# Quantised layer at four slots a tile beside projections at every second slot, without unread products

## The reference

```python
h = tok(x)                        # relu(x W0') * (x W1'), then Wo', 256 -> 512 -> 256
h = ln(h + attn0(h))              # 16 heads of 16, mask |i - j| <= 64, softmax
h = ln(h + ffn0(h))               # quantised: gate, up (256 -> 1024), down (1024 -> 256)
h = ln(h + attn1(h))              # 16 heads of 16, causal
h = ln(h + moe(h))                # 8 experts (256 -> 1024 -> 256), top 2, then its own layer norm

def act_quant(x):                 # by row
    scale = 127.0 / clip(max(abs(x)), EPS)
    return clip(round(x * scale), -128, 127) / scale
def weight_quant(w):
    scale = 1.0 / clip(mean(abs(w)), EPS)
    return clip(round(w * scale), -1, 1) / scale
def ffn0(x):
    g, u = bitlinear(x, w_gate), bitlinear(x, w_up)
    return bitlinear(square(relu(g)) * u, w_down)
# moe: softmax of x wg, top 2, a running count per expert gives each row its place, at most CAP rows each
```

## Time and profile before

| | |
|---|---|
| Median of 3 runs | 1079.14 us (1068.04 to 1080.44) |
| The profiled execution | 1079.0 us |
| Its span, first to last instruction | 1077.1 us |
| Busy: PE, DVE, ACT, POOL | 914.4, 546.3, 417.6, 295.2 us |
| Mean granted TensorE clock | 0.926 |

### The profile page before, as it was taken

The page is one execution under the profiler, slowest core; times in us unless marked ns, Lnnn a source line. Parts: engine busy times, 40 slices in busy tenths (PEclk is TensorE's granted clock), DMA queues, the critical chain, the costliest instruction groups (busy, mean ns, idle before and its releaser), DMA issues. The chain is left out here.

```text
span 1077.1 us, 14453 instructions
## 1 busy us (share of the span) xinstructions
PE 914.4 (85%) x5031; PEld 561.6 (52%) x5054; DVE 546.3 (51%) x2104; ACT 417.6 (39%) x717; POOL 295.2 (27%) x364
## 2 busy tenths in 40 slices
PE   6897999878879879888987979867999999999940
PEld 3454455534535534434533525344687777777830
DVE  1257434678778678757785767541021112111137
ACT  1315334476475566565635545501311211121003
POOL 5101322413413413301324342335021122112232
PEclk9998999999989999988988988978999999999975
DMA  9882341542253252430564360153142353243242
GB/s 352 146 186 31 32 80 21 60 40 35 27 60 38 32 52 36 48 38 2 60 88 72 38 104 21 57 196 97 40 96 52 118 132 66 77 123 69 25 102 78
DMA packets 57511, 81.49 MB, mean 76 GB/s; under 512 B 6624, under 2 KB 51041, under 8 KB 55008
## 3 DMA queue, kind: packets, MB, share of 16 engines
q1 hardware_dynamic: 49520, 70.48, 32.9%
q0 software_dynamic: 7296, 9.47, 5.2%
q10 hardware_dynamic: 624, 0.63, 0.2%
HBM read 35.37 MB, written 19.68 MB: 51 GB/s over the span
## 5 line engine op out<-in xcount | busy, mean ns | idle before, releaser
L1099 DVE CUSTOM_DVE_ANT_0 junk<-ps,maskb 128x256 bf16<-128x256 f32 (+4 forms) x512 | 206.3, 434 | 96.6 <-PE ps L809 93.2
L630 ACT ACTIVATE probs<-ps 128x512 f32<-128x512 f32 (+1 forms) x304 | 159.2, 550 | 118.5 <-PE ps L832 115.4
L1551 PE MATMUL ps<-dxT,qs 128*128 128x320 f32 x512 | 139.6, 433 | 1.3 <-DVE dxT L1617 1.3
L1563 PE MATMUL ps<-ks,hTe 128*128 128x256 f32 x640 | 139.3, 379 | 0.0
L1587 ACT ACTIVATE hTe<-ps,qs 128x640 f32<-128x640 f32 x64 | 50.8, 794 | 204.6 <-PE ps L1551 204.6
L1563 PEld LDWEIGHTS ps<-ks,hTe 128*128 128x128 f32 x640 | 121.3, 190 | 16.1
L1507 POOL DMA_INDIRECT mixed_rows<-ysb,ids x40 | 61.7, 1543 | 228.8 <-DVE ysb L1637 225.9
L832 PE MATMUL ps<-qs,ks 99*128 99x256 bf16 (+4 forms) x512 | 104.1, 289 | 23.4 <-DVE nmax L1099 13.7
L1551 PEld LDWEIGHTS ps<-dxT,qs 128*128 128x128 f32 x512 | 97.2, 190 | 41.5 <-DVE dxT L1617 1.7
L809 PE MATMUL ps<-ks,qs 96*128 96x256 bf16 (+4 forms) x512 | 106.2, 290 | 11.1 <-DVE nmax L1099 5.4
L848 PE MATMUL ps<-probs,vaug 128*32 128x256 f32 (+4 forms) x1024 | 92.2, 434 | 10.5 <-issue 5.7
(11 more groups left out here) (183 smaller groups left out, 1242.3 us busy)
## 6 DMA issues: line engine op xcount, KB each, us to landing
qs<-parts SPq DMA_DIRECT2D x96, 128.0 KB, 4.7
ks<-parts SPq DMA_DIRECT2D x96, 128.0 KB, 7.4
qs<-w SPq DMA_DIRECT2D x8, 1024.0 KB
ks<-w SPq DMA_DIRECT2D x8, 1024.0 KB, 4.9
dispatched_rows<-att SPq DMA_DIRECT2D x8, 650.0 KB, 16.9
ks<-dispatched_rows SPq DMA_DIRECT2D x4, 650.0 KB, 7.4
x_sb<-xT SPq DMA_DIRECT2D x8, 256.0 KB, 4.2
mixed_rows<-h SPq DMA_DIRECT2D x4, 512.0 KB
```

What stands on the lines that cost most here:

```text
L630: act.activation(probs_of(u)[:, heads[0]:heads[-1] + 1, :], turned_bank((u, half, i))[:, 0:len(heads) * w].rearrange("p (j n) -> p j n", n=w),
L1099: ins = dve.tensor_tensor_reduce(out=junk[:, AT["s", (u, half, i)][0], a * (hi - lo):(a + 1) * (hi - lo)], in0=score_bank((u, half, i))[:, ...
L1551: ins = mm(bank(2 * (n % 2) + c)[:, 0:HC], w1s[:, e % 2, k, m * P:(m + 1) * P], dxT[:, e % 2, k, c * HC:(c + 1) * HC], start=(k == 0), sto ...
L1563: ins = mm(bank(4 + n % 2)[:, 0:D], hTe[:, e % 2, m, t * P:(t + 1) * P], w2s[:, e % 2, m, :], start=(m == 0), stop=(m == MH - 1))
```

## The change

The quantised layer's tiles come four slots apart instead of two, and VectorE reads an up product one slot after TensorE makes it. Projections 2 to 7 take every second slot (`stretched`) and start 8 or 10 slots earlier, so that they run beside the quantised layer (3 to 6), the token layer (2) and the sends (7). The values get a third buffer, and `junk` loses the place of the bank that it never uses. All of `keep_busy` and the six products ahead of the experts go; where the wait stood behind them it now stands ahead of opening the bank.

```diff
+NV = 3
 DENSE = (
-    ("wq", 2, 12), ("qkv", 1, 14), ("tok", 2, 22), ("tok", 3, 34), ("qkv", 2, 46), ("o", 0, 54), ("ffn", 0, 60),
-    ("qkv", 3, 77), ("o", 1, 85), ("ffn", 1, 91), ("qkv", 4, 108), ("o", 2, 117), ("ffn", 2, 123), ("qkv", 5, 140),
-    ("o", 3, 149), ("ffn", 3, 155), ("qkv", 6, 172), ("o", 4, 181), ("gate", 0, 185), ("route", 0, 187), ("send", 0, 196), ("qkv", 7, 204), ("o", 5, 213),
...
+    ("wq", 2, 12), ("qkv", 1, 14), ("tok", 2, 22), ("tok", 3, 34), ("qkv", 2, 38), ("o", 0, 54), ("ffn", 0, 60),
+    ("qkv", 3, 66), ("o", 1, 85), ("ffn", 1, 91), ("qkv", 4, 98), ("o", 2, 117), ("ffn", 2, 123), ("qkv", 5, 130),
+    ("o", 3, 149), ("ffn", 3, 155), ("qkv", 6, 162), ("o", 4, 181), ("gate", 0, 185), ("route", 0, 187),
+    ("send", 0, 196), ("qkv", 7, 196), ("o", 5, 213), ("gate", 1, 217), ("route", 1, 219), ("send", 1, 228),
...
-STEPS = {"tok": 12, "qkv": 8, "o": 6, "ffn": 16, "gate": 2, "route": 9, "send": 4, "bias": 2, "wq": 4}
-FQT, FIRST_TILE, PER_TILE = 3, 3, 2
-QUANT, TURN, DOWN, STATS, NORM = 2, 3, 4, 5, 6
+STEPS = {"tok": 12, "qkv": 8, "o": 6, "ffn": 25, "gate": 2, "route": 9, "send": 4, "bias": 2, "wq": 4}
+FQT, FIRST_TILE, PER_TILE = 3, 3, 4
+HIDDEN = 1
+QUANT, TURN, DOWN, STATS, NORM = 4, 6, 7, 8, 9
+def stretched(phase, i, c):
+    return 2 * c if phase == 'qkv' and 2 <= i else c
-        SCHED.setdefault(_at + _c, []).append((_phase, _i, _c))
+        SCHED.setdefault(_at + stretched(_phase, _i, _c), []).append((_phase, _i, _c))
-            vaug = sb2("vaug", [P, 2, NT, VW])
+            vaug = sb2("vaug", [P, NV, NT, VW])
-            junk = sb2("junk", [P, BANKS, S], BF16)
+            junk = sb2("junk", [P, BANKS - 1, S], BF16)
 # ScalarE, values of a projection
-                                if i < 2:
-                                    act.wait_ge(prep_pool, 8)
+                                if i < NV:
+                                    act.wait_ge(prep_pool, 6 + NV)
+                                elif k == 0:
+                                    act.wait_ge(pv_mm, NG * NT * (i - NV + 1))
 # ScalarE, scaling of a tile
-                            t = tile_at(c, 1)
+                            t = tile_at(c, HIDDEN + 1)
 # TensorE
-                            if u == 0 and half == 0:
-                                pe.wait_ge(mask_done, 1)
-                                keep_busy(o, 24)
...
-                            o = d_open(("ffn", i, "fqT"))
-                            keep_busy(o, 12)
-                            o = o.bitcast(BF16)
                             pe.wait_ge(fq_done, i + 1)
+                            o = d_open(("ffn", i, "fqT")).bitcast(BF16)
...
-                                o = d_open(("ffn", i, f"f{t}"))
-                                keep_busy(o, 3)
-                                o = o.bitcast(BF16)
                                 pe.wait_ge(fq2_done, NT * i + t + 1)
+                                o = d_open(("ffn", i, f"f{t}")).bitcast(BF16)
...
+                            pe.wait_ge(chosen, i + 1)
                             o = d_open(("route", i, "cnt"))
-                            keep_busy(o, 10)
-                            pe.wait_ge(chosen, i + 1)
...
-                            if i == 0:
-                                keep_busy(o, 12)
                             pe.wait_ge(w_sum, i + 1)
...
-                    pe.wait_ge(routed, B)
-                    keep_busy(bank(V_BANK), 34)
 # VectorE
-                            t = tile_at(c, 0)
+                            t = tile_at(c, HIDDEN)
                             if t is not None:
                                 hidden(i, t, 0)
-                            t = tile_at(c, 1)
+                            t = tile_at(c, HIDDEN + 1)
                             if t is not None:
                                 hidden(i, t, 1)
                                 hidden_scale(i, t)
 # TensorE, experts
-                    for _ in range(6):
-                        mm(bank(0), identb[:, :], maskb[:, 0:S], start=True, stop=True)
```

More of the change, by code:

```diff
@@ L97 @@
     ("tok", 0, -20), ("qkv", 0, -8), ("tok", 1, 0), ("bias", 0, 1), ("bias", 1, 2), ("wq", 0, 4), ("wq", 1, 8),
-    ("wq", 2, 12), ("qkv", 1, 14), ("tok", 2, 22), ("tok", 3, 34), ("qkv", 2, 46), ("o", 0, 54), ("ffn", 0, 60),
-    ("qkv", 3, 77), ("o", 1, 85), ("ffn", 1, 91), ("qkv", 4, 108), ("o", 2, 117), ("ffn", 2, 123), ("qkv", 5, 140),
-    ("o", 3, 149), ("ffn", 3, 155), ("qkv", 6, 172), ("o", 4, 181), ("gate", 0, 185), ("route", 0, 187), ("send", 0, 196), ("qkv", 7, 204), ("o", 5, 213),
-    ("gate", 1, 217), ("route", 1, 219), ("send", 1, 228), ("o", 6, 245), ("gate", 2, 249), ("route", 2, 251), ("send", 2, 271), ("o", 7, 278), ("gate", 3, 282), ("route", 3, 284), ("send", 3, 293))
-STEPS = {"tok": 12, "qkv": 8, "o": 6, "ffn": 16, "gate": 2, "route": 9, "send": 4, "bias": 2, "wq": 4}
-FQT, FIRST_TILE, PER_TILE = 3, 3, 2
-QUANT, TURN, DOWN, STATS, NORM = 2, 3, 4, 5, 6
+    ("wq", 2, 12), ("qkv", 1, 14), ("tok", 2, 22), ("tok", 3, 34), ("qkv", 2, 38), ("o", 0, 54), ("ffn", 0, 60),
+    ("qkv", 3, 66), ("o", 1, 85), ("ffn", 1, 91), ("qkv", 4, 98), ("o", 2, 117), ("ffn", 2, 123), ("qkv", 5, 130),
+    ("o", 3, 149), ("ffn", 3, 155), ("qkv", 6, 162), ("o", 4, 181), ("gate", 0, 185), ("route", 0, 187),
+    ("send", 0, 196), ("qkv", 7, 196), ("o", 5, 213), ("gate", 1, 217), ("route", 1, 219), ("send", 1, 228),
+    ("o", 6, 245), ("gate", 2, 249), ("route", 2, 251), ("send", 2, 271), ("o", 7, 278), ("gate", 3, 282),
+    ("route", 3, 284), ("send", 3, 293),)
+STEPS = {"tok": 12, "qkv": 8, "o": 6, "ffn": 25, "gate": 2, "route": 9, "send": 4, "bias": 2, "wq": 4}
+FQT, FIRST_TILE, PER_TILE = 3, 3, 4
+HIDDEN = 1
+QUANT, TURN, DOWN, STATS, NORM = 4, 6, 7, 8, 9
 def tile_at(c, off):
@@ L529, in _ @@
                     pool.wait_ge(prep_pool, 6)
-                    for i in range(2):
+                    for i in range(NV):
                         pool.memset(vaug[:, i, :, 0:H * SLOT].rearrange("p t (h s) -> p t h s", s=SLOT)
@@ L790, in t_open @@
                         return opened("t", key)
-                    def keep_busy(o, n):
-                        for _ in range(n):
-                            mm(o, identb[:, :], maskb[:, 0:S], start=True, stop=True)
                     def scores(u, half):
                         q = block_of(u)
+                        if u % 8 == 0 and half == 0:
+                            pe.wait_ge(stack_in[q % NR], STACKED * (q // NR + 1))
                         t = u % NT
@@ L801, in scores @@
                             o = s_open((u, half, i))
-                            if u == 0 and half == 0:
-                                pe.wait_ge(mask_done, 1)
-                                keep_busy(o, 24)
-                            if u % 8 == 0 and half == 0 and i == 0:
-                                pe.wait_ge(stack_in[q % NR], STACKED * (q // NR + 1))
                             for a, j in enumerate(heads):
@@ L1039, in dense @@
                                 pe.wait_ge(prep, 2)
-                            o = d_open(("wq", i, "one"))
-                            if i == 0:
-                                keep_busy(o, 12)
                             pe.wait_ge(w_sum, i + 1)
-                            mm(o[:, 0:4], ones, wsc[:, 4 * i + 12:4 * i + 16], start=True,
+                            mm(d_open(("wq", i, "one"))[:, 0:4], ones, wsc[:, 4 * i + 12:4 * i + 16], start=True,
                                stop=True).then_inc(d_full(("wq", i, "one"))[0], 1)
@@ L1096, in maximum @@
                         for i, heads in enumerate(score_heads(u, half)):
+                            b = AT["s", (u, half, i)][0]
                             dve.wait_ge(*s_full((u, half, i)))
@@ L1099, in maximum @@
                                 ins = dve.tensor_tensor_reduce(
-                                    out=junk[:, AT["s", (u, half, i)][0], a * (hi - lo):(a + 1) * (hi - lo)],
+                                    out=junk[:, b - (b > V_BANK), a * (hi - lo):(a + 1) * (hi - lo)],
                                     in0=score_bank((u, half, i))[:, a * (hi - lo):(a + 1) * (hi - lo)], in1=mask,
```

4 lines of the change are left out of this document (2 added, 2 removed).

## The result

The changed kernel takes 1063.97 us in the median of four runs (1063.28 to 1064.37), the kernel before, beside it on the same chip, 1079.79 us: a ratio of 0.988, 95% interval 0.984 to 0.993. That is 1.2% faster, where 3.7% was forecast; the time lies in the range, but among the cases of "within 2%". The profiled execution has a span of 1061.4 us against 1077.1.

A forecast was written before the change was run, and what follows sets the result against it. The stretches were taken as bound by no engine but by a chain in program order; 23.8 + 6.6 + 7.2 + 2.4 + 1.5 + 4.4 - 6.0 = 39.9 us won gave about 1039 us, range 1020 to 1070.

The forecast's parts named there:

- within 2%: Whole kernel: outcomes not told apart from no change, the limit being 1057.6 us; chance 0.26.
- the stretches: Four 32-slot stretches, 234.6 us in sum: VectorE's share rises from 0.77 to 0.86, 23.8 us won.
- Projection 2 beside token layer 3: Slots 38 to 53: TensorE full and its work the same, third buffer and earlier stack copies free; 0 us.
- taken back by the next wait on VectorE: Closing warning: gains in front of a stretch may be lost to VectorE, whose 546 us of work stay; no size given.
- the stretch brings nothing: Rival: VectorE's share in the four stretches stays 0.77, only 16.1 us won, 1063 us; chance 0.24.
- The lockstep: In the four stretches, banks held one slot longer make TensorE and VectorE wait for each other, 64 us at most.
- The clock at the turns and the unread products before them: Four quantised layers' turns: 6.6 us won without twelve unread products before each, 6.0 lost to TensorE starting at half clock.
- Routing: Routing counts: without ten unread products before each, 3.0, 2.0 and 2.2 us won, in sum 7.2.
- The weights' means: Before the weights' mean: without twelve unread products, 2.4 us won.
- projection 7 beside the sends: At the sends: projection 7's transposes and first two units fill TensorE's wait for probabilities, 4.4 us won.
- The experts' start: Before the experts: without six unread products of 2.5 us at half clock, 1.5 us won.
- The clock rival: Rival: without unread products TensorE runs the stretches mostly at 1.2 GHz, 1112 us at a mean grant of 0.60; chance 0.09.

The follow-up runs named there:

- half change: Changed kernel with projections 2 to 6 unstretched at their old places, quantised layers still at four slots a tile: 1062.88 us, ratio 0.991.
- both moves: Changed kernel, projection 2 unstretched at slot 46, projections 3 to 6 from 72, 104, 136, 168, output projections, quantised layers, gates, routings two slots later: 1037.91 us.

## Why the prediction was wrong, step by step

**The step that failed** is the cost of the stretched layer outside its stretches. The sum costed what happens inside the stretches and took what stands behind them as unchanged; it had no line for the output projections. With 25 steps instead of 16 the layer's residual, statistics and normalisation move next to the heads on VectorE's in-order queue, and the projection's early end lets TensorE run ahead to the same place. Measured: +18.0 us, of which the half change showed 8.6. TensorE's waits for the heads are 4.9 us of it (none before) and those for row copies 4.2 more. A second term that was put at nothing belongs here: "Projection 2 beside token layer 3" left its own slots as they were (39.7 against 39.6 us), as forecast, but with it back in its place the output projection behind it took 2.4 us less. The same term let the stack copies go out earlier for nothing, looking only at what stands behind them in SP's queue; the row copy that waits is issued by ScalarE.

Without the 18.0 us of the output projections the difference is -33.7 against the -39.9 forecast, and with both causes reduced the kernel took 1037.9 us. That this is near the forecast 1039 is luck: it is another order, with another sum (output projections still +7.5, stretches, counted two slots later, -30.6 against the -23.8 forecast). The prediction's last sentence named the danger, "taken back by the next wait on VectorE", but gave it no place and no price: none of its rivals was this one. The case with a like time, "the stretch brings nothing" (1063), did not happen.

**The stretches** were right: 20.2 of 23.8 us, shares of 0.83 and, with both moves, 0.86. The lockstep did not come: the longest bank wait was 1.4 us, and its removal made things worse.

**The clock at the turns and the unread products before them.** At the fourth layer VectorE was done at 455.99 (455.30 + 0.69) and the transposes started at once:

```profile
456.06 1.03 PE L888 MATMUL ps<-identb,work 128*128 128x128 bf16 x8 [1.05 <-DVE work L1271]
```

0.07 us behind, where it was 4.9, and at half clock, as forecast (the grant from 454.0 to 459.9 is 0.50). Slots 155 to 158 won 3.7 us; the first three heads lost 1.4, 0.3 and 0. The forecast for the four, in order, was +1.5, +0.5, +0.6 and -3.2: together -2.0, forecast -0.6.

**Routing** was over-sized: 2.5 us instead of 7.2. The choice ended at 541.34 in the changed kernel, and the count came only at

```profile
542.37 0.21 PE L1025 MATMUL ps<-mk,trib 128*128 128x64 bf16 x1 [0.92 <-DVE nmax L1094]
```

behind scores that wait for VectorE's maxima. VectorE works 16.7 us of those 19.6 (15.75 of 20.2 before): the products had stood in place of waiting for VectorE, whose share was the thing to price.

**The weights' means** gave 4.0 instead of 2.4 (put back, they cost 4.0), **projection 7 beside the sends** 6.1 instead of 4.4, and the wait of the earlier trace rows is gone. **The experts' start** gave nothing: 401.5 and 402.1 us to the end, against 1.5 won in the sum.

**The clock rival** did not happen: the stretches ran at 0.93 to 0.98. The unread products had kept nothing that mattered: in the old order the time is 1.002 without them.

## What to carry to other kernels

When a stage is spread over more slots, list where its last steps now stand on each in-order queue, and what stands next behind them: here most of the stage's gain was kept only when the waits of the consumer on its new edge were gone. When one engine's work is spread evenly, look at the handover behind it, and try to move the consumer as well: two slots were enough here. List the transfers too, since a copy that TensorE needs can come to stand behind others that now go out close to it. Try to let VectorE read a product one step after it is made, even at the price of a bank held longer; in this kernel that paid.

## What the runs showed of the hardware

VectorE's normalisation step (L1157, 128x256 from SBUF to SBUF) took 0.39 to 0.42 us in every one of the 385 cases, over all kernels of this document, in which no instruction of GpSimd ran beside it. The half change has two of them in front of its second output projection (minimum, median, maximum in ns):

```profile
L1157 DVE TENSOR_SCALAR h<-att,mv,rstd x2: 408/410/411, 272.1 to 272.4; 128x256 f32<-128x256 f32 x2
```

The 1.35 us in the changed kernel, above, are two at 0.7, beside these two mask selections of GpSimd; the 2.63 us are two at 1.3 to 1.4, beside GpSimd's additions (a bias to `h`, laid in a projection's last two steps) in the half change:

```profile
350.63 0.64 POOL L554 TENSOR_SCALAR_AFFINE_SELECT probs<-probs 128x512 f32<-128x512 f32 x1
351.21 0.69 POOL L557 TENSOR_SCALAR_AFFINE_SELECT probs<-probs 128x512 f32<-128x512 f32 x1
```

```profile
348.81 2.54 POOL L579 TENSOR_TENSOR h<-h,ar 128x512 f32<-128x512 f32 x2
```

The Trainium skill, "GPSIMD Engine Reference", in its table of specifications, says that GpSimd shares its SBUF interfaces with VectorE and that instructions of VectorE in a two-port mode, or with two inputs from SBUF, contend with it. The durations fit this; whether L1157 runs in such a mode no view says, and that this contention is the reason was only read from them. What stood beside the same two instructions changed with the order and made their price 0.7, 1.4 or 2.6 us, in front of a consumer that waits.
